# 32x32 transposes on VectorE for the attention sums and the maxima, sequences written out, stages re-placed, one shared PSUM bank

## The reference

```python
qkv = x @ w_attn + b_attn                       # x: (8, 512, 128) f32
att = softmax(where(causal, q @ k.T / sqrt(8), -inf))   # per head, 512 x 512
x1 = layernorm(x + (att @ v) @ w_proj + b_proj)
x_prev = x1 shifted by one row
r = sigmoid((mu_r*x1 + (1-mu_r)*x_prev) @ W_r.T)
k = (mu_k*x1 + (1-mu_k)*x_prev) @ W_k.T
out = layernorm(x1 + r * (square(relu(k)) @ W_v.T))
```

## Time and profile before

| | us |
|---|---|
| median of 3 runs | 401.3 (395.59 to 401.83) |
| profiled execution | 401.56 |
| its span, first to last instruction | 399.8 |
| busy: PE / DVE / ACT / POOL | 324.1 / 307.2 / 267.4 / 164.2 |

### The profile page before, as it was taken

One profiled execution on the slowest core, in us unless ns is written; L12 is line 12 of the kernel. 1 busy time (PEld: TensorE's weight loads), 2 busy tenths in 40 slices (PEclk: granted clock), 3 DMA queues, 4 the chain that ended last, 5 costly groups with the idle time before them and its releaser, 6 DMA issues. The chain is left out here.

```text
span 399.8 us, 9188 instructions
## 1 busy us (share of the span) xinstructions
PE 324.1 (81%) x2647; PEld 132.3 (33%) x2647; DVE 307.2 (77%) x1345; ACT 267.4 (67%) x513; POOL 164.2 (41%) x244
## 2 busy tenths in 40 slices
PE   4478789889888988888969989799888888987853
PEld 1212233233333424343422424234332423332433
DVE  2598789789797888798854897889887898971354
ACT  3204777777868886787734877687867886787541
POOL 8101343343553443544441435443534434534512
PEclk9999999999999999999975999999999999998966
DMA  2601321140014201140101401042012310001000
GB/s 79 191 3 33 104 58 35 36 133 18 15 45 108 55 28 55 47 121 28 56 6 40 119 28 53 5 121 64 1 55 74 90 30 29 1 3 29 0 27 26
DMA packets 28880, 20.46 MB, mean 51 GB/s; under 512 B 2920, under 2 KB 28840, under 8 KB 28840
## 3 DMA queue, kind: packets, MB, share of 16 engines
q1 hardware_dynamic: 28840, 20.00, 18.1%
HBM read 4.72 MB, written 2.10 MB: 17 GB/s over the span
## 5 line engine op out<-in xcount | busy, mean ns | idle before, releaser
L845 DVE CUSTOM_DVE_ANT_0 masked<-mx_ps,mask_wide 128x384 f32<-128x384 f32 (+3 forms) x512 | 222.7, 486 | 44.4 <-PE mx_ps L485 39.6
L689 ACT ACTIVATE probs<-ex_ps 128x512 f32<-128x512 f32 x308 | 175.2, 595 | 56.5 <-PE ex_ps L501 55.5
L501 PE MATMUL ex_ps<-q_st,k_st 64*128 64x512 bf16 (+1 forms) x492 | 113.8, 309 | 26.1 <-ACT probs L689 25.4
L1096 POOL TENSOR_SCALAR_AFFINE_SELECT probs<-probs 128x512 f32<-128x512 f32 x128 | 79.2, 636 | 132.5 <-ACT probs L689 132.3
L485 PE MATMUL mx_ps<-k_st,q_st 64*128 64x512 bf16 (+3 forms) x512 | 121.4, 319 | 14.9 <-DVE m_max L845 9.4
L525 PE MATMUL pv_ps<-probs,vals 128*32 128x512 f32 (+3 forms) x1024 | 97.0, 453 | 0.0
L501 PEld LDWEIGHTS ex_ps<-q_st,k_st 64*128 64x128 bf16 x492 | 31.8, 95 | 121.6 <-ACT probs L689 78.7
L485 PEld LDWEIGHTS mx_ps<-k_st,q_st 64*128 64x128 bf16 x512 | 33.5, 95 | 34.0 <-DVE m_max L845 27.4
L845 DVE DVE_READ_ACCUMULATOR2_ANT m_max<- 128x1 f32 x512 | 42.2, 82 | 0.0
L1134 POOL TENSOR_TENSOR mixT<-mix_cur,mix_prev 128x512 f32<-128x512 f32 x14 | 17.8, 1274 | 35.6 <-ACT mix_prev L738 35.6
L675 ACT ACTIVATE m_rows<-sh_ps 8x512 bf16<-8x512 f32 x32 | 18.5, 579 | 20.8 <-PE sh_ps L511 20.8
(11 more groups left out here) (133 smaller groups left out, 367.3 us busy)
## 6 DMA issues: line engine op xcount, KB each, us to landing
q_st<-q_part SPq DMA_DIRECT2D x48, 128.0 KB
k_st<-k_part SPq DMA_DIRECT2D x48, 128.0 KB, 2.4
x_in<-in_L_attn_x_dram SPq DMA_DIRECT2D x8, 256.0 KB, 2.9
x_res<-in_L_attn_x_dram SPq DMA_DIRECT2D x8, 256.0 KB, 3.0
out_dram<-o_sb SPq DMA_DIRECT2D x7, 256.0 KB, 2.4
q_st<-m_rows SPq DMA_DIRECT2D x32, 8.0 KB
q_st<-zero_b SPq DMA_DIRECT2D x8, 32.0 KB
out_dram<-o_sb SPq DMA_DIRECT2D x2, 128.0 KB, 1.8
```

Of the source, the lines that this page charges most:

```text
L501: last = mm(ps[:, at:at + n], k_st[par][side, slot, t * P:(t + 1) * P], q_st[par][side, slot, t * P:T], start=True, stop=True)
L689: act.activation(dst, src, ACT.Exp, scale=SCALE).then_inc(exp_done, 1)
L845: last = dve.tensor_tensor_reduce(out=masked[u % len(masked)][:, at:at + n], in0=mx_ps[MX_BANK[u]][:, at:at + n], in1=mask_wide[:, T - n:T ...
L1096: pool.affine_select(out=blocks, in_=blocks, compare_op=ALU.is_ge, fill=0.0, base=0, pattern=[[0, HG], [1, P]], channel_multiplier=-1).the ...
```

## The change

- **Maxima.** `max_parts` now runs directly behind a group's last maxima. Behind the two splits DVE transposes 32x32 blocks of a 128 x 32 bf16 tile into `m_turn`. The PE matmuls, the ACT copy and a shared bank fall away. SP now needs 4 DMAs a group (`ROW_DMAS`), of 2 KB each.
- **Sums.** DVE transposes `pv_ps` (128 x 512 f32 in PSUM) by 32x32 blocks into `y_rows` (`rows_back`), takes reciprocals (`denominators`); POOL multiplies (`normalise`); DVE transposes `yn` (128 x 512 f32 in SBUF) into `ynT` (`channels_back`). The ACT copies and all 12 PE transposes a sequence of this part fall away.
- **Banks.** One shared bank instead of two, three banks of logits instead of two. The last groups no longer borrow banks.
- **Moved.** `q_rest` and `k_rest` from DVE to POOL, for which ACT writes a second full copy (`q_full`, `k_full`); the division's multiply and the second residual from DVE to POOL; the first normalisation from DVE to ACT, for which POOL computes a second `neg_mean` and `shift`. The factor 0.5 of the gate goes into the weights.
- **Order.** All 8 sequences are written out, with new tables. The maxima run 18 steps ahead (`LEAD`), not 20. In the prologue ACT issues the keys' stacks and SP the queries', and semaphores of the constants are split. The residual sum and store, the biases' loads and SP's order have new places.

```diff
-PE_AT = {"maxT0": 2, "xT": 3, "q": 6, "k": 8, "Y1": 10, "maxT1": 13, "ynT": 14, "proj": 16, "v": 19, "maxT2": 22,
-         "x1T": 25, "Y0": 29, "kT": 32, "maxT3": 34, "r": 35, "kv": 37}
-ACT_AT = {"maxT0": 2, "xT": 3, "q": 5, "sums1": 8, "k": 9, "q_mid": 10, "k_mid": 13, "maxT1": 13, "ynT": 13, "norm2":
-          16, "norm2b": 19, "v": 21, "maxT2": 22, "share0": 26, "share1": 27, "sums0": 28, "share2": 30, "share3": 31,
-          "kT": 32, "maxT3": 33, "r": 34}
-DVE_AT = {"aggregates2": 0, "q": 8, "Y1": 9, "k": 10, "add1": 16, "stats1": 18, "stats1b": 18, "aggregates1": 19,
-          "norm1b": 22, "norm1": 23, "Y0": 29, "gated": 37, "add2": 38, "stats2": 39, "stats2b": 39}
-
-POOL_AT = {"deviations2": 0, "residual": 1, "q_low": 2, "k_low": 3, "deviations1": 6, "mix1": 7, "mix0": 9, "squares":
-           9}
-EX_BANKS = 2
+LEAD = 18
+ROW_DMAS = P // 32
+PE_AT = {"xT": 0, "q": 2, "k": 9, "v": 12, "proj": 16, "x1T": 27, "kT": 33, "r": 37, "kv": 39}
+ACT_AT = {"xT": 0, "q": 2, "q_full": 6, "k": 9, "k_full": 9, "q_mid": 10, "v": 12, "k_mid": 14, "norm2": 7, "norm2b": 13, "norm1": 23, "norm1b": 25, "share0": 27, "share1": 29, "share2": 30, "share3": 30, "kT": 34,
+          "r": 36}
+DVE_AT = {"aggregates2": 3, "rows1": 8, "rden1": 10, "ynT": 13, "add1": 16, "stats1": 18, "stats1b": 18, "aggregates1": 18, "rows0": 28, "rden0": 31, "gated": 39, "stats2": 2}
+POOL_AT = {"deviations2": 2, "q_rest": 4, "k_rest": 9, "q_low": 11, "yn1": 8, "k_low": 13, "residual": 36, "deviations1": 21, "mix1": 29, "mix0": 30, "yn0": 30, "squares": 35, "add2": 38}
+SP_AT = {"q_high": 6, "k_high": 9, "q_mid": 11, "q_low": 12, "k_mid": 14, "k_low": 14, "store": 15, "x_res": 2, "x_in": 20}
+MX_BANKS, EX_BANKS = 3, 3
...
+            def stack_maxima(group):
+
+                b, g = divmod(group, SLOTS)
+                wait(sp, m_turned, group + 1)
+                rows = q_st[b % 2][MAX_BAND::MAX_STEP, 2 * g:2 * g + 2, :].rearrange("j p (t a r) -> j (p t) a r", t=NT, r=32)
+                for a in range(ROW_DMAS):
+                    sp.dma_start(rows[:, :, a, :], m_turn[group % 2][a * 32:(a + 1) * 32, :]).then_inc(rows_stacked, 16)
...
-            def max_rows(name, step_b, n):
-                wait(act, rows_stacked, n * 16)
-                copy(name, step_b, m_rows[:, :])
-
-            def sums(b, j):
-
-                wait(act, pv_done, b * SLOTS + (2 * j + 2))
-                if j == 1:
-                    wait_full(act, "Y0", b)
-                elif has_prev(b):
-                    wait_full(act, "Y1", b)
-                act.activation(yT[:, :], pv_ps[:, :], ACT.Copy).then_inc(yT_done, 1)
...
+            def fulls(i, step_b, b):
+
+                name, _, full, _, bias = q_and_k[i]
+                wait(act, rest_done[i], b - 1)
+                act.activation(full[:, :], sh_ps[:, :], ACT.Identity, bias=bias[:, 0:1]).then_inc(sh_read, 1)
...
+            def attention_normed(b, tiles):
+
+                wait(act, h2_done, b)
+                wait(act, shift_ready[0], b + 1)
+                for t in tiles:
+                    act.activation(x1[:, t, :], h1[:, t, :], ACT.Identity, scale=rstd[0][:, t:t + 1],
+                                   bias=shift[0][:, t:t + 1]).then_inc(x1_done, 1)
...
+                wait(dve, m_lo, group + 1)
+                wait(dve, rows_stacked, (group - 1) * ROWS_STACKED)
+                dve.transpose(m_turn[group % 2][:, :], m_part[:, :, :, :].rearrange("p s a i -> p (s a i)")
+                              ).then_inc(m_turned, 1)
+
+            def rows_back(b, j):
+
+                wait(dve, pv_done, b * SLOTS + 2 * j + 2)
+                wait(dve, yn_done, 2 * b + j)
+                dve.transpose(y_rows[:, :, :].rearrange("p a w -> p (a w)"), pv_ps[:, :]).then_inc(rows_done, 1)
+
+            def denominators(b, j):
+                wait(dve, rows_done, 2 * b + j + 1)
+                dve.reciprocal(rden[:, :, :], y_rows[:, :, 2 * HD:2 * HD + 2]).then_inc(rden_done, 1)
+
+            def channels_back(step_b, b):
+
+                wait(dve, yn_done, 2 * b + 2)
+                if b:
+                    wait_full(dve, "proj", step_b - 1)
+                dve.transpose(ynT[:, :], yn[:, :, :, :, :].rearrange("p a j s d -> p (a j s d)")).then_inc(ynT_done, 1)
...
+            def rests(i, step_b, b):
+
+                name, part, full, rest = q_and_k[i]
+                wait(pool, high[i], b + 1)
+                wait(pool, mid[i], b)
+                wait(pool, low[i], b)
+                wait_read(pool, name, step_b)
+                pool.tensor_tensor(rest[:, :], full[:, :], part[:, 0, :], ALU.subtract).then_inc(rest_done[i], 1)
...
+            def normalise(b, j):
+
+                wait(pool, rden_done, 2 * b + j + 1)
+                if j == 0:
+                    wait(pool, ynT_done, b)
+                pool.tensor_tensor(yn[:, :, j, :, :], y_rows[:, :, 0:2 * HD].rearrange("p a (s d) -> p a s d", s=2),
+                                   rden[:, :, :].unsqueeze(3).to_broadcast([P, T // 32, 2, HD]), ALU.mult
+                                   ).then_inc(yn_done, 1)
...
+            def ffn_added(step_b, b):
+
+                wait_read(pool, "kv", step_b)
+                wait(pool, x1_done, b * NT + NT)
+                wait(pool, o_done, b * NT)
+                wait(pool, bn[1], b * NT)
+                pool.tensor_tensor(h2[:, :, :], gated[:, :, :], x1[:, :, :], ALU.add).then_inc(h2_done, 1)
```

More of the change, by code:

```diff
@@ L334, in block_kernel, with stack_part @@
+        def stack_part(eng, which, part, b):
+            st, part_of, stacked = ((q_st[b % 2], q_part, q_stacked), (k_st[b % 2], k_part, k_stacked))[which]
+            wait(eng, (high, mid, low)[part][which], b + 1)
+            for band, band_part in enumerate((Q_PARTS, K_PARTS)[which]):
+                if band_part == part:
+                    eng.dma_start(st[band::BANDS, :, :], part_of[:, part, :]).then_inc(stacked, 16)
+        x1T_ps = kv_ps = [mx_ps[0], ex_ps[0]]
         proj_ps = kT_ps = [mx_ps[1], ex_ps[1]]
@@ new lines, in _ @@
+            pe.wait_ge(ones_stacked[1], 16)
+            for unit in range(UNITS):
+                logits(unit)
+                if unit + LEAD < UNITS:
+                    maxima(unit + LEAD)
+                b, at = divmod(unit, PER_SEQ)
+                if at % STEPS in PV_AT and unit >= STEPS:
+                    weighted_values(unit // STEPS - 1, PV_ORDER[PV_AT[at % STEPS]])
+                if has_next(b):
+                    if at == PE_AT["xT"]:
+                        x_transposed(b, b + 1)
+                    if at == PE_AT["q"]:
+                        queries(b)
+                    if at == PE_AT["k"]:
+                        keys(b)
+                    if at == PE_AT["v"]:
+                        values(b)
+                if has_prev(b):
+                    if at == PE_AT["proj"]:
+                        project(b, b - 1)
+                    if at == PE_AT["x1T"]:
+                        x1_transposed(b, b - 1)
+                    if at == PE_AT["kT"]:
+                        ffn_in(b, b - 1)
+                    if at == PE_AT["r"]:
+                        ffn_gate(b, b - 1)
+                    if at == PE_AT["kv"]:
+                        ffn_out(b, b - 1)
@@ new lines, in highs @@
+                act.activation(part[:, 0, :], sh_ps[:, :], ACT.Identity, bias=bias[:, 0:1]).then_inc(high[i], 1)
+            def fulls(i, step_b, b):
+                name, _, full, _, bias = q_and_k[i]
+                wait(act, rest_done[i], b - 1)
+                act.activation(full[:, :], sh_ps[:, :], ACT.Identity, bias=bias[:, 0:1]).then_inc(sh_read, 1)
+            def mids(i, step_b, b):
+                name, part, _, rest, _ = q_and_k[i]
+                if b == 0:
+                    wait_read(act, name, step_b)
+                else:
+                    wait(act, rest_done[i], b)
@@ L813, in _ @@
             last_b = NB - 1
-            sums(last_b, 1)
             ffn_normed(last_b - 1, range(NT))
-            for half in range(2):
-                cols = half_cols(half)
-                act.wait_ge(ynT_half, half + 1)
-                act.activation(ynT[:, cols], ynT_ps[half][:, 0:HALF], ACT.Copy).then_inc(ynT_copied, 1)
             for half in range(2):
@@ new lines, in _, with first_rests, first_lows @@
+            q_and_k = (("q", q_part, q_rest, b_q), ("k", k_part, k_rest, b_k))
+            def first_rests(i):
+                name, part, rest, bias = q_and_k[i]
+                dve.wait_ge(high[i], 1)
+                wait_full(dve, name, -1)
+                dve.scalar_tensor_tensor(out=rest[:, :], in0=sh_ps[:, :], scalar=bias[:, 0:1], in1=part[:, 0, :],
+                                         op0=ALU.add, op1=ALU.subtract).then_inc(sh_read, 1)
+            def first_lows(i):
+                _, part, rest, _ = q_and_k[i]
+                dve.wait_ge(mid[i], 1)
```

(13 more changed lines are left out.)

882 lines of the change are left out of this document (368 added, 514 removed).

## The result

The changed kernel takes 350.6 us (median of 4 runs, 348.5 to 352.0) against 401.6: a ratio of 0.880, 95% interval 0.866 to 0.893. The ratio compares undisturbed executions alone, which for the kernel before are 395.6 and 401.3 us, so it lies nearer to 1 than 350.6 / 401.6 = 0.873. The profiled execution has a span of 350.3 us against 399.8.

What follows compares the result with a forecast made beforehand. PE's in-order list was taken to set the pace, with VectorE's load just beside it. Six middle sequences -32.6 us, prologue -3, first sequence -2, last -1, tail -1: -39.6 from 401.6 gives 362 us; range 350 to 384.

Steps and rivals of the forecast that it cites:

- rival 2: Smoother than thought: both neighbouring engine pairs decouple, period 37.6 us, total 352 us; chance 0.10.
- Transposes: New VectorE block transposes: three of 128 x 512 f32 at 0.69 us and four small at 0.25 a sequence.
- rival 4: Slower than before: f32 block transposes run near the reciprocal's rate, 464 us at 5.7 us each; chance 0.03.
- rival 1: VectorE's idle time stays (378 us, chance 0.14) or its transposes cost near double (376 us, chance 0.08).
- Period: Ordinary sequence falls from 43.34 to 39.3 us, VectorE 35.6 busy plus 3.7 idle; bounds 37.6 and 41.9.
- Loop: Writing out all sequences removes the hardware loop's turn, with its gap and slow clock: 7.9 us less.
- Prologue: Start of kernel: stacks issued from two queues 1.5 us, two steps of maxima fewer 1.5; together -3 us.
- Tail: After the last sequence: an ACT copy and PE transposes and copies become four half transposes on DVE, -1 us.
- GpSimd's cover: GpSimd's added 5.5 us a sequence costs 0 if its in-order waits miss the masks; otherwise each about 1 us.
- SyncE: 16 DMAs of maxima become 4; k's low part lands near step 20, needed at step 22, so cost 0.
- rival 3: Late stacks or masks: 3 to 4 steps late, PE stands about 3.5 us a sequence, 386 us; chance 0.06.
- Shared bank at step 0: PE waits at `xT` until VectorE has read `kv` from the one shared bank: about 0.5 us a sequence.

Runs made afterwards that it cites:

- experiment 2: The changed kernel with two banks of logits instead of three, the eighth bank left unused: 373.6 us, ratio 0.940 to the kernel before.
- Experiment 6: The changed kernel with first keys and values in free banks of logits, weights from SyncE's queue, one late FFN sum on VectorE: 346.4 us against 352.9.
- experiment 4: The kernel before, written out, with three banks of logits and one shared bank instead of two and two: 391.5 us against 390.3 for the written-out kernel.

## Why the prediction was right, and where it was off

**Direction and mechanism** held: the period fell because VectorE's and PE's loads fell and the third bank uncoupled PE from ScalarE, and VectorE became the bound, with PE close behind. Its size was off in one term above all. The forecast's own band, 354 to 370 us with a chance of 0.55, missed; the range held by 0.6 us because it took in rival 2, and because two terms at the ends erred the other way.

- **Transposes.** Taken 0.69 and 0.25 us; measured 0.71 and 0.21. The choice of the nearest row (a pass over 128 x 512 from PSUM) was right, and with it rival 4 and the price of rival 1 fell away; the prediction's other estimate, 1.24 us, is 0.53 too high for this form.
- **Loads.** PE 34.3: measured 33.5 to 35.0. VectorE 35.6: 34.9, or 36.2 in long sequences. ScalarE 32.0: 31.3 to 32.1. GpSimd 25.3: 24.8. All within 3%. For VectorE there is luck in it: the mean over the six sequences is 35.7, but only since the long passes, which the prediction didn't have, put 1.1 to 1.3 us on three of them.
- **Period, the step that failed.** 39.3 against 36.5 to 37.9. "I let 4.4 become 2, leave 1.0 for other stages, and add 0.7 of new waits" gave VectorE 3.7 us of idle time; it has 1.5 to 1.7. The wait for maxima became 0.5, not 2. The 3.7 are what two banks of logits leave (3.6, experiment 2): I had credited the bank to PE's idle time and then carried too little of it over to VectorE. The six sequences between 65.34 and 288.38 us took 37.2 on the mean: (39.3 - 37.2) x 6 = 13 us, more than the whole error. This is rival 2, with chance 0.10 and 352 us.
- **First and last sequence.** Taken -2 and -1. What is left of the eight sequences around those six went from 74.1 to 69.1 us, -5.
- **Loop.** 7.9 us: 8.3 in the two sequences; 7 to 11 for writing out as a whole.
- **Prologue.** Taken -3; measured +0.8. The step that failed is the part on the banks: it looked for the price of the one shared bank only at `kv` and `xT` in a sequence, and not in the prologue, where queries, keys and values now follow each other through it, each behind VectorE's reading of the one before. Experiment 6 gave 3.3 us back, and experiment 4 shows the same loss, 3.0 us at the first mark, in the kernel before.
- **Tail.** Taken -1, measured +0.1. The halved transposes are there, but GpSimd's sum, moved from VectorE, delayed the last mask. The prediction had named the risk for the masks (`add2` at 38) and costed it at nothing; in the last sequence there is no cover.
- **GpSimd's cover.** Costed 0 on the condition that its waits don't reach the masks. They don't. But its passes hold VectorE's small passes, 0.3 or 1.4 us a sequence, of which no row of before gave a hint that I had read: there the same two forms have means of 0.23 and 0.20 us, against 0.27 and 0.37, and GpSimd is 5 us a sequence less busy.
- **SyncE.** Keys were said to land near step 20, needed at 22. They land late in two of the six sequences, where PE waits 1.2 and 1.3 us. This is rival 3's mechanism and one of the prediction's own signs of being wrong, at a third of rival 3's size. VectorE waits 0.5 us for maxima in such a sequence, so little of it arrives there; that the three banks of maxima are the cover is argued, not shown.
- **Shared bank at step 0.** Taken 0.5, measured 0.6.

Put together by runs: 401.6 to 390.3 by writing out (11), to 373.6 by the transposes and moved stages with two banks (17), to 350.6 by the third bank (23). By the ratios, of which the first is the least certain, it is 7 to 8, 16 and 24. The order matters: taken first, the third bank gives nothing (experiment 4).

## What to carry to other kernels

When work is moved off an engine, ask which buffers it frees as well: here the third bank of logits was worth 23 us, and the transposes and moved stages without it 17. When passes are moved to GpSimd, look at what VectorE does beside them. Follow each freed wait to the engine that sets the pace, since a stall taken off one engine's row must be taken off the next one's too. And where a shared bank replaces two, walk through the prologue and the last sequence by themselves: what a steady sequence covers lies bare there.
